# Attention of layer 1 in rounds: the next scores moved ahead by three projections, two softmaxes moved ahead of the last addition

## What is computed

```python
x = x + _L0_attn_ref(_layernorm(x), L0_attn_w_project, L0_attn_w_out)
x = x + _L0_ffn_ref(_layernorm(x), ...)
x = x + _L1_attn_ref(_layernorm(x), L1_attn_w_qkv, L1_attn_w_proj)   # 16 heads, 4 key/value heads, head size 128
x = x + _L1_ffn_ref(_layernorm(x), ...)                              # 2048 hidden, 4-bit gate/up/down

# _L1_attn_ref, with s = 4 (our b) and b = 512 (our positions)
qkv    = jnp.einsum('sbh,ph->sbp', x, w_qkv)
scores = jnp.einsum('bhsd,bhtd->bhst', q, k) * scale     # 4 x 4 for each position and head
out    = jnp.einsum('bhst,bhtd->bhsd', softmax(scores), v)
return jnp.einsum('sbe,he->sbh', out, w_proj)
```

## Time and profile before

| | before |
|---|---|
| median of 3 runs | 1190.35 us (1189.95 to 1190.75) |
| the profiled execution | 1194.26 us, its span 1192.5 us |
| PE matmul / DVE / ACT / POOL busy | 84% / 72% / 42% / 26% of the span |
| mean granted TensorE clock | 0.927 of full speed |
| layer 1's attention | about 600 to 925 us in the span |

### The profile page before, as it was taken

How to read it: one execution, slowest core, us unless ns; L and a number is a source line. 1 busy time by engine, 2 the same in 40 slices (tenths; PEclk the granted TensorE clock), 3 DMA queues, 4 the chain that set the end, 5 groups by cost and what they waited for, 6 DMA issues and landing times. The chain is left out here.

```text
span 1192.5 us, 19875 instructions
## 1 busy us (share of the span) xinstructions
PE 1005.9 (84%) x6885; PEld 588.9 (49%) x6960; DVE 857.1 (72%) x1556; ACT 498.4 (42%) x972; POOL 311.4 (26%) x337
## 2 busy tenths in 40 slices
PE   3698989888788798797487898898989799999997
PEld 1344545445444454353134474474657465556554
DVE  5677767643999899999967754746582776777766
ACT  2154444354464564646334313314230344444443
POOL 3243424531532524333320202203135400000000
PEclk9799989998899798898789898898897999999999
DMA  6622222101001000010000000001001000000000
GB/s 172 112 73 90 64 81 67 58 2 45 1 1 44 1 27 18 0 45 1 0 18 6 23 11 16 21 2 26 11 24 46 22 1 18 1 18 0 18 1 18
DMA packets 37088, 35.87 MB, mean 30 GB/s; under 512 B 8585, under 2 KB 33417, under 8 KB 37009
## 3 DMA queue, kind: packets, MB, share of 16 engines
q1 hardware_dynamic: 35728, 33.79, 9.8%
q10 hardware_dynamic: 1280, 1.05, 0.7%
HBM read 27.28 MB, written 6.29 MB: 28 GB/s over the span
## 5 line engine op out<-in xcount | busy, mean ns | idle before, releaser
L883 DVE TENSOR_REDUCE bm<-ps 128x4 f32<-128x512 f32 x160 | 102.1, 684 | 33.4 <-PE ps L603 31.7
L782 ACT ACTIVATE pt<-ps 128x1024 f32<-128x1024 f32 (+1 forms) x96 | 82.1, 882 | 72.5 <-PE ps L679 71.9
L1753 DVE TENSOR_TENSOR qk_lo<-ps,qk_hi 128x512 bf16<-128x512 f32 x80 | 54.9, 687 | 67.1 <-ACT qk_hi L1646 60.8
L2001 ACT ACTIVATE g<-ps 128x512 f32<-128x512 f32 x64 | 38.2, 597 | 134.1 <-PE ps L1948 107.4
L156 POOL TENSOR_TENSOR mag_w<-stage 128x512 f32<-128x512 fp8e4 x24 | 26.4, 1100 | 224.7 <-DVE stage L143 224.7
L2051 DVE SCALAR_TENSOR_TENSOR g<-g,ps 128x512 f32<-128x512 f32 x64 | 44.0, 688 | 54.5 <-ACT g L2001 54.2
L599 PE MATMUL ps<-ks,qs 96*128 96x512 bf16 (+3 forms) x256 | 66.7, 314 | 12.4 <-DMA ks<-scratch_k 7.7
L1646 ACT ACTIVATE qk_hi<-ps 128x512 bf16<-128x512 f32 x80 | 47.8, 599 | 69.4 <-PE ps L1515 69.4
L547 POOL TENSOR_SCALAR_AFFINE_SELECT pt<-pt 128x256 f32<-128x256 f32 (+1 forms) x96 | 47.2, 498 | 110.9 <-ACT pt L782 110.3
L1515 PE MATMUL ps<-wp_hi,oT_hi 128*128 128x256 bf16 x256 | 71.1, 278 | 5.0 <-DVE oT_lo L1746 5.0
L1964 PE MATMUL ps<-ew_hi,it_hi 128*128 128x256 bf16 x256 | 69.8, 273 | 6.1 <-DVE it_lo L2067 6.1
(11 more groups left out here) (272 smaller groups left out, 2840.9 us busy)
## 6 DMA issues: line engine op xcount, KB each, us to landing
qs<-scratch_q SPq DMA_DIRECT2D x64, 64.0 KB, 2.6
ks<-scratch_k SPq DMA_DIRECT2D x48, 64.0 KB, 2.6
q_next<-in_w_qkv SPq DMA_DIRECT2D x4, 768.0 KB, 4.4
X<-in_x SPq DMA_DIRECT2D x4, 512.0 KB, 7.0
w_next<-in_router_w SPq DMA_DIRECT2D x4, 512.0 KB, 3.7
w_next<-in_expert_w SPq DMA_DIRECT2D x4, 512.0 KB, 4.6
p_next<-in_w_proj SPq DMA_DIRECT2D x4, 512.0 KB, 5.4
out<-X SPq DMA_DIRECT2D x8, 256.0 KB, 2.3
```

The source lines that it names most:

```text
L782: act.activation(pt[kt][:, heads[0]:heads[-1] + 1, :], src, ACT.Exp).then_inc(s_exp, 1)
L883: ins = dve.tensor_reduce(bm[:, 2 * g + i // 5, 4 * (i % 5):4 * (i % 5) + 4], src.rearrange("p (k q) -> p k q", k=4), AX_X, ALU.max)
L1753: dve.tensor_tensor(qk_lo[:, k, h, :], bank(QK_BANK[m]), qk_hi[:, k, h, :], ALU.subtract).then_inc(s_qklo, 1)
```

## The change

TensorE's second argument of `project` becomes a list of batches. The next round's scores and the turn follow the projection of batch 0 alone, and batches 1 to 3 come behind them. On DVE, `softmax_b` of blocks 0 and 1 of the next round is finished in front of `add(g, 1)` (for round 0 in front of the loop), `add(g, 0)` moves behind `softmax_a` of block 2, and in the chunks the low copies of the outputs stand first, followed for c = 1 and 2 by `softmax_b` of block c + 1. The number of instructions and the arithmetic stay the same; ACT, POOL and the DMA queues keep their programs.

```diff
-                def project(g, pair):
+                def project(g, batches):
                     pe.wait_ge(s_olo, NB * OC * (g + 1))
                     pe.wait_ge(s_ohi, NB * OC * (g + 1))
-                    for b in (2 * pair, 2 * pair + 1):
+                    for b in batches:
...
-                    project(g, 0)
+                    project(g, (0,))
                     if not last:
                         scores(g + 1)
                     if g + 2 <= G:
                         turn(g + 2)
-                    project(g, 1)
+                    project(g, (1, 2, 3))
...
+                def probabilities(g, blocks):
+                    for j in blocks:
+                        for _ in softmax_b(g, j):
+                            pass
+
                 scores_shifted(0, (0, 1))
                 x_low(1)
                 scores_shifted(0, (2, 3))
+                probabilities(0, (0, 1))
...
                     for c in range(NB):
-                        main, steps = softmax_b(g, c), SMB
+                        main, steps = iter(()), 0
                         if c:
-                            main, steps = chain(main, outputs_lo(g, c - 1)), SMB + OC
+                            main, steps = outputs_lo(g, c - 1), OC
+                        if c in (1, 2):
+                            main, steps = chain(main, softmax_b(g, c + 1)), steps + SMB
                         interleave(chain(main, dq.decode(dve, NU2 * g + c, c % 2)), steps + DEC, tiles, 0 if last else QK)
...
                     if last:
                         down_decoded((0, 1))
-                    add(g, 0)
-                    if last:
+                        add(g, 0)
                         down_decoded(range(2, DOWN_FIRST))
                     else:
                         scores_shifted(g + 1, (0, 1))
                         x_low(g + 2)
-                        scores_shifted(g + 1, (2, 3))
+                        scores_shifted(g + 1, (2,))
+                        add(g, 0)
+                        scores_shifted(g + 1, (3,))
+                        probabilities(g + 1, (0, 1))
                     add(g, 1)
```

## The result

The changed kernel took 1156.01 us in the median of 4 runs (1153.05 to 1156.73), the kernel before beside it 1190.55 us (1189.95 to 1192.47). The ratio is 0.969, with a 95% interval of 0.9663 to 0.9717: 3.1% faster. I had forecast 1161.0 us in a range from 1154 to 1168. The ratio, applied to the 1190.35 us shown ahead, gives 1153.5 us, half a microsecond outside the range: the direction and the mechanism were right, the gain that I forecast was too small (29.3 us forecast, 34.5 to 37 measured, by the two medians or by the ratio). The miss is a narrow one: the interval, applied in the same way, runs from 1150.2 to 1156.7 us, on both sides of the range's lower end.

What follows compares the result with a forecast made beforehand. TensorE and VectorE were taken to wait for each other in a ring, neither full. Three stretches saving 30.9 us less 1.65 us at round 0's start gave 29.3 us: 1161.0 us, range 1154 to 1168.

Steps and rivals of the forecast that it cites:

- c = 1: Chunk 1 of a round's attention: VectorE's list ends at 9.43 us, and TensorE has no wait before its outputs.
- the three stretches that I had named: Layer 1 attention, rounds 0 to 2, from the chunk behind outputs 0 to the projection: each falls from 40.37 to 30.0 us.
- c = 2: Chunk 2: VectorE, without idle time, ends its 7.61 us list at 17.04 us; TensorE waits 0.9 us.
- c = 3: Chunk 3, without a softmax: four copies and two tiles end at 20.64 us; TensorE has waited since 19.2.
- c = 4: Last chunk: 2.1 us from last copy to its first matmul, then 7.3 us to the projection, which starts at 30.0.
- The low bound: Low end of the forecast: no lowered clock in chunks 3 and 4, stretch 27.8 us, kernel 1153.7 us.
- Rival B: Attention chunks: full clock throughout, giving the forecast's low end, 1154 us; chance 0.10 beyond that low end.
- The tail: End of rounds 0 to 2, from the projection on: moved addition and softmaxes fit VectorE's idle time, cost nothing.
- the later ones are wider: Tiles delayed on VectorE: margin before TensorE needs the bank is 1.5 us at tile 11, wider for later tiles.
- Round 0's start: Before round 0's first tile: two softmaxes with no projection to hide under, 1.65 us lost.
- Rival C: Attention rounds: rotation saves only block 1's softmax, 2.15 us a round, 4.8 us in all, 1185.5 us; chance 0.07, with other half gains.
- Rival A: Chunks 2 to 4: TensorE's clock stays at half, 10.2 us a chunk, kernel slower at 1196.5 us; chance 0.04.

Runs made afterwards that it cites:

- experiment 3: Changed kernel with idle VectorE writes added behind the softmax of chunk 2 in rounds 0 to 2: three writes 1164.66 us, six writes 1175.46 us.
- experiment 1: Changed VectorE order with TensorE's old order: 1157.49 us; kernel before with only TensorE's new order of projection and scores: 1195.06 us.
- experiment 2: Changed kernel without softmaxes in advance, copies in front: 1190.4 us; changed kernel with softmaxes in advance, copies behind the softmax: 1179.63 us.

## Why the prediction missed its size

- *Where the time would come from:* right. The windows put 38.4 of 38.7 us into the three stretches that I had named.
- *VectorE's order:* right to 3%. Forecast for the end of c = 1 and c = 2 and for the last copy of c = 3, counted from the stretch's start: 9.43, 17.04, 20.64. Measured: 9.20, 16.55, 20.22 (802.76 - 782.54).
- *The waits:* forecast 0, 0.9 and 1.4 us before outputs 1 to 3. Measured 0, 0.87 and about 1.6: chunk 3 ended at 801.15, and outputs 3 took 2.9 instead of 1.33 us.
- *The step that failed:* the two terms of c = 4, which I took from rows of before with a lowered clock. "I take 2.1" for the time from the last copy to chunk 4: measured 1.37 (802.76 to 804.13). "I take 7.3, near the row, since a wait of 1.4 us still lies in front": measured 5.99. Together 2.0 us a round; another 0.4 is DVE's. The stretch is 27.58, not 30.0 us, and three times the difference is 7.3 us. The windows of the changed kernel show the reason: at this place copies that come 1.6 us late do not lower the clock (1.00 in all three stretches), and experiment 3 shows that later ones do. The low bound, 27.8, was built with the full clock; the changed kernel in its second execution and the one with VectorE's order alone had stretches of 27.79 to 27.80 us, and the execution shown lay 0.2 below. Rival B was the case, and 0.10 was too little for it.
- *A slip in the sum:* 40.37 - 30.0 is 10.37, and three times that 31.1, not 30.9 us.
- *The margins:* right. The tail costs nothing, even with TensorE's old order (experiment 1): DVE waits 2.7 to 2.9 us before `add(g, 1)`, where I forecast about 2. No wait for `qk_lo` appears inside a chunk of rounds 1 and 2. But "the later ones are wider" was too bold: three writes, 1.96 us, were enough for a wait of 0.48 us inside chunk 3, so the margin there is about 1.5 us too. And PE does have pauses between projection and values, inside the scores; they were there before as well.
- *Round 0's start:* forecast 1.65 us lost; PE's wait for the first tile grew from 3.27 to 4.76 us, the window by 1.24.
- *Last round:* forecast zero, within 0.8; 1.0 us gained (19.87 to 18.88). No run isolates the cause.
- *Rival C* (a rotation gains only what is moved out, 4.8 us) was not the case: the softmaxes alone gained 12.9 us. But rotating alone gains next to nothing, as experiment 2 shows. What I gave as the reason against the rival, that the change takes the ready copies out from behind the tile wait, pays only once the softmaxes are out of the chunk too.
- *Rival A* did not occur. The Trainium skill ("TensorE: Matmul & The Clock Gate", section on a second failure mode) had it that small pauses between matmul groups set the clock swinging. In the changed kernel PE pauses several times in each chunk, 0.16 to 0.87 us, at a granted clock of 1.00; the measurement decides, for pauses of this length and spacing. Experiments 2 and 3 show the clock falling behind longer ones.

Left open: what exactly makes the clock fall. Copies 2.9 us late did it in one round and not in two others, while in the kernel before copies 2.5 us late did it each time; no run tells what else decides.

## What to carry to other kernels

Where in-order engines hand results round in a ring, list for each waiting instruction *all* its inputs and ask of each whether it is made in front of or behind the next wait of the engine that makes it; mending one of two inputs may show nothing, and is no proof that the idea is wrong. An idle stretch elsewhere in the round is where the second input can be made in advance. And cost a remaining wait at the clock that it leaves behind: rows behind long waits overprice what follows a short one, so keep the full-clock sum as a case of its own.

## What the runs showed of the hardware

The granted clock held at 1.00 through PE waits of 0.16 to 0.87 us around each chunk, with the last copy up to 1.6 us late, and at 1.00 behind one single wait of 1.87 us. Single waits of 2.20 to 3.13 us were each followed by matmuls at half clock. It fell in all three rounds when six idle writes made PE wait 1.59 us inside chunk 3 and then put the last copy 3.4 us behind it: outputs and chunk took 4.90 + 7.94 us against 2.65 + 6.22 in the same kernel without the idle writes. The cost of lateness is therefore not linear: the first 1.96 us of idle writes cost a stretch 1.96 us in two rounds and 3.43 in the third; the second 1.96 us cost another 3.2 to 4.4 us.
